# The next tile's score products set singly between value products, instead of in a block

## The reference

```python
def _L0_xattn_ref(q, k, v, Wq, bq, Wk, bk, Wv, bv):   # q: 256x512, k = v = context: 25088x512
    qp = einsum('bsd,ed->bse', q, Wq) + bq            # 256 x 128
    kp = einsum('bsd,ed->bse', k, Wk) + bk            # 25088 x 128
    vp = einsum('bsd,ed->bse', v, Wv) + bv
    z = sigmoid(einsum('bqe,bke->bqk', qp, kp) / sqrt(128))
    return einsum('bqk,bkd->bqd', z, vp)

x = x + _L0_xattn_ref(_layernorm(x), ctx_1024, ctx_1024, ...)
x = x + _L0_attn_ref(_layernorm(x), ...)
x = x + _L0_ffn_ref(_layernorm(x), ...)
```

## Time and profile before

| | us |
|---|---|
| median of 3 runs | 576.66 (576.39 to 577.11) |
| the profiled execution | 576.42 |
| its span, first to last instruction | 574.6 |
| PE busy | 569.0 (99%) |
| PEld busy | 477.3 (83%) |
| DVE busy | 456.3 (79%) |
| ACT busy | 402.2 (70%) |
| granted TensorE clock | 1.000 |

### The profile page before, as it was taken

How to read it: one execution, slowest core, us unless ns; L and a number is a source line. 1 busy time by engine, 2 the same in 40 slices (tenths; PEclk the granted TensorE clock), 3 DMA queues, 4 the chain that set the end, 5 groups by cost and what they waited for, 6 DMA issues and landing times.

```text
span 574.6 us, 8074 instructions
## 1 busy us (share of the span) xinstructions
PE 569.0 (99%) x3010; PEld 477.3 (83%) x3010; DVE 456.3 (79%) x494; ACT 402.2 (70%) x542; POOL 1.7 (0%) x7
## 2 busy tenths in 40 slices
PE   8999999999999999999999999999999999999998
PEld 5888888888888888888888888888888887877887
DVE  6987878787878797879788988787878798887742
ACT  6776767676767787778777787776777784697321
POOL 1000000000000000000000000000000000000000
PEclk9999999999999999999999999999999999999999
DMA  9667787767677877787678777677687742100201
GB/s 329 224 198 244 236 248 228 230 216 244 211 233 243 265 244 229 248 270 243 222 254 254 249 230 256 219 222 223 216 277 236 221 147 110 38 1 2 75 0 38
DMA packets 33239, 115.90 MB, mean 202 GB/s; under 512 B 4080, under 2 KB 4784, under 8 KB 32944
## 3 DMA queue, kind: packets, MB, share of 16 engines
q1 hardware_dynamic: 32768, 115.05, 63.2%
q10 hardware_dynamic: 432, 0.33, 0.2%
HBM read 114.84 MB, written 0.52 MB: 201 GB/s over the span
## 4 chain that ended last, share of the span: by engine, by line
PE 96%; ACT 2%; DVE 1%; issue 0%; POOL 0%; POOLq 0%
PE ps L959 95%; ACT w L548 1%; PE ps L1042 0%; PE ps L1208 0%; PE ps L1295 0%; DVE zl L652 0%; ACT zh L384 0%; PE ps L1167 0%; DVE aTs L847 0%; DVE st L737 0%; DVE sm_s L824 0%; DVE x_s L735 0%; PE ps L1177 0%; ACT zf L415 0%; ACT qk L384 0%
## 5 line engine op out<-in xcount | busy, mean ns | idle before, releaser
L959 PE MATMUL ps<-nh,zh 128*128 128x512 f32 x388 | 142.7, 390 | 0.0
L959 PE MATMUL ps<-nh,zl 128*128 128x512 f32 x388 | 142.6, 389 | 0.1
L959 PE MATMUL ps<-nl,zh 128*128 128x512 f32 x388 | 142.5, 389 | 0.0
L652 DVE TENSOR_TENSOR zl<-zf,zh 128x1024 fp32r<-128x1024 f32 x49 | 60.1, 1226 | 80.5 <-ACT zh L384 80.5
L642 DVE TENSOR_TENSOR nl<-rawn,nh 128x1024 fp32r<-128x1024 f32 x96 | 114.2, 1220 | 0.9 <-issue 0.5
L631 DVE TENSOR_TENSOR tl<-rawt,th 128x1024 fp32r<-128x1024 f32 x96 | 113.0, 1217 | 0.8 <-ACT th L384 0.7
L384 ACT ACTIVATE nh<-rawn 128x1024 fp32r<-128x1024 f32 x96 | 100.4, 1057 | 13.2 <-DMA rawn<-in_ctxn 12.6
L384 ACT ACTIVATE th<-rawt 128x1024 fp32r<-128x1024 f32 x96 | 96.2, 1053 | 1.0 <-DMA rawt<-in_ctxt 1.0
L415 ACT ACTIVATE zf<-ps 128x512 f32<-128x512 f32 x98 | 58.4, 598 | 54.5 <-PE ps L959 48.7
L959 PEld LDWEIGHTS ps<-nh,zl 128*128 128x128 f32 x388 | 72.8, 188 | 15.6 <-DVE zl L652 0.5
L959 PEld LDWEIGHTS ps<-nh,zh 128*128 128x128 f32 x388 | 72.6, 188 | 15.4 <-ACT zh L384 0.4
(11 more groups left out here) (176 smaller groups left out, 613.8 us busy)
## 6 DMA issues: line engine op xcount, KB each, us to landing
rawn<-in_ctxn SPq DMA_DIRECT2D x97, 512.0 KB, 6.6
rawt<-in_ctxt SPq DMA_DIRECT2D x96, 512.0 KB, 5.0
h_s<-in_wg SPq DMA_DIRECT2D x4, 512.0 KB, 6.8
h_s<-in_wu SPq DMA_DIRECT2D x4, 512.0 KB, 7.3
wds<-in_wd SPq DMA_DIRECT2D x4, 512.0 KB, 4.0
raw<-in_ctxt SPq DMA_DIRECT2D x2, 512.0 KB, 8.7
h_s<-in_wvt SPq DMA_DIRECT2D x2, 512.0 KB, 7.3
wq_s<-in_wq SPq DMA_DIRECT2D x1, 1024.0 KB, 10.6
```

The source lines that it names most:

```text
L652: e.tensor_tensor(zl[b % 2][:], zf[:], zh[b % 2][:], ALU.subtract).then_inc(*s.zl.mark(b))
L959: return e.matmul(o, w, x, start=start, stop=stop)
```

## The change

The block `scores(b)` goes out of the loop. Instead `values(b)` issues the score products of tile b + 1 singly: one after each of its last twelve value products, in the same order as before (quarter h, then i). The semaphore waits go with them (`score_waits`), and so do the marks of s. The mark av now comes with the last value product, one score product before the end of the pairs. The last tile's scores keep their block. No product, load, transfer or buffer is added or taken away.

```diff
+            def score_waits(b, i, j):
+                if (i, j) == (0, 0):
+                    e.wait_ge(*s.kph.of(b))
+                    e.wait_ge(*s.zf.of((b - 1, 1)))
+                if (i, j) == (2, 0):
+                    e.wait_ge(*s.kpl.of(b))
+
             def scores(b):
-                e.wait_ge(*s.kph.of(b))
-                e.wait_ge(*s.zf.of((b - 1, 1)))
                 for j in range(4):
                     for i in range(3):
-                        if (i, j) == (2, 0):
-                            e.wait_ge(*s.kpl.of(b))
+                        score_waits(b, i, j)
                         m = score(b, i, j)
                     if j % 2:
                         m.then_inc(*s.s.mark((b, j // 2)))
@@ in values(b), in the loop over j = 2, 3, r = 0, 1, i = 0, 1, 2
                             m = value(b, j, r, i)
-                m.then_inc(*s.av.mark(b))
+                            if (j, r, i) == (3, 1, 2):
+                                m.then_inc(*s.av.mark(b))
+                            if b < NB - 2:
+                                k, h = i, 2 * (j - 2) + r
+                                score_waits(b + 1, k, h)
+                                m = score(b + 1, k, h)
+                                if (k, h % 2) == (2, 1):
+                                    m.then_inc(*s.s.mark((b + 1, h // 2)))
@@ the loop over the tiles
             for b in range(1, NB - 1):
-                scores(b)
                 keys(b + 1)
                 if b < NB - 2:
                     values(b)
```

## The result

The changed kernel takes 580.34 us (579.97 to 580.49), before 576.66: the ratio is 1.006, 95% interval 1.0048 to 1.0071. It is 3.7 us slower. The profiled execution has a span of 578.5 us where before had 574.6. It lies inside the stated range, but not in the case that I held likeliest; it is the rival "the wide products never recover their rhythm", for which the text had worked out 580.7.

A forecast was written before the change was run, and what follows sets the result against it. The tensor engine's own rhythm, 9.62 us a tile, was taken as the bound. Profiled 576.42 us + 0 for the pairs + 0.5 for the start stall = 576.9, or 577.2 against the median; stated 577.1, range 573.0 to 581.2.

The forecast's parts named there:

- the case that I held likeliest: Whole kernel: pairs cost what the blocks did, only the start stall adds; 575.9 to 577.4 us, chance 0.47 including case 3.
- the wide products never recover their rhythm: Mixed half: single scores keep values at 233.3 ns, pair 353.3, +3.8 us, 580.7 with the stall; slower, chance 0.31.
- What bounds the kernel: Whole stream: only the tensor engine's own rhythm counts, 9.62 us a tile; any added stall shows in full.
- Part 1, the pair: Mixed halves of 47 tiles, 564 value-score pairs: each costs 346.7 ns as before, so 0 us.
- the short distance is 113 and the value behind it takes 233: Step pricing one pair from rows at block ends: 346.7 ns, exactly the 226.7 + 120.0 of before.
- The bounds, 340.0 and 355.0: Limits in ns for one pair in the mixed half: -3.8 to +4.7 us over 564 pairs.
- The forecast's own sign: Mixed half: the forecast is wrong if the pair differs from 346.7 ns by more than 2 ns.
- Faster, the loads are hidden: Mixed half: score 113.3 and value 226.7, pair 340.0 ns, -3.8 us, 573.2 with the stall; chance 0.20.
- Case 3: Wide products behind each score block: the 0.03 us tail vanishes too, -0.9 us, 576.0 with the stall; inside the forecast's 0.47.
- The estimate from figures: Pair by the skill page's formulas: load 106.7 ns, products 109 and 216, pair 325 ns in either order, change worth 0.
- Part 2, the waits: Scores' waits moved 2.7 us earlier: slack from tile 2 on; in tile 0 a wait on DVE's low keys, 0.53 us once.
- Part 3, the marks: Moved marks: end-of-values about 1.3 us later at no cost; first sigmoid sooner, worth nothing as rounding awaits the second mark.

The follow-up runs named there:

- first: Changed kernel, except that tile 1's scores stay a block behind tile 0's values (no start stall): 579.2 us, ratio 1.0041.
- third: Changed kernel with tile 1's scores as a block and the three products of each value sum in another order: 579.4 us, ratio 1.0043.
- eleventh: Changed kernel with tile 1's scores as a block; mixed half has its first two scores together, then single ones, a value last: 581.31 us, ratio 1.0076.
- twelfth: Changed kernel with tile 1's scores as a block; one score behind every second value from the eighth, last three scores at the end: 580.07 us, ratio 1.0053.
- seventh: Kernel before with 32 unused bytes per partition ahead of all tiles of the stream, moving its operands together: 576.75 us, ratio 0.9999.
- eighth: Kernel before with 32 unused bytes ahead of zh and zl alone, shifting the value products' weights against their streams: 583.88 us, ratio 1.0122.
- sixth: Changed kernel with tile 1's scores as a block; mixed half in groups of six values, then six scores: 577.49 us, ratio 1.0015.
- second: Changed kernel with tile 1's scores as a block; mixed half in groups of two values, then two scores: 576.74 us, ratio 0.9996.
- fifth: Changed kernel with tile 1's scores as a block; mixed half in groups of three values, then three scores: 577.4 us, ratio 1.0015.

## Why the prediction was right or wrong

**What bounds the kernel: right.** The stream is PE's own rhythm and nothing else; a change of 6.7 ns in the distance of two products shows in full in the kernel's time, and so does a stall of half a microsecond.

**Part 1, the pair: wrong by 6.7 ns, and with it the point forecast.** The step that failed is "the short distance is 113 and the value behind it takes 233". I took the row for the first score of a block and the row for the first wide product behind a block, and set them side by side as if each pair began from the settled state in which those rows stand. The first pair does: 113 and 232. The two behind it, of the same sizes, come to 118 and 241, 120 and 236, before the row starts again; that they begin from what the pair before left is my reading of it. Pairs in a row are a state of their own, 353.3 ns on the mean, that no row of before shows. The forecast's own sign, a pair within 2 ns of 346.7, says that it was wrong. The bounds, 340.0 and 355.0, held the pair; that the range held the time is owed to the rival that was kept in it, not to the forecast. Why the row has three places no run shows. The rival had the size, 353.3, but its parts were off: 233.3 and 120.0 there, 236.3 and 117.0 on the mean here. Its period of 9.70 was 0.02 too high, because the keys behind the last pair recover with one dear product (236) and not with five: they gave 19 ns back.

**The rivals.** "Faster, the loads are hidden" is out: a score did cost 113 to 120, so up to seven nanoseconds were won there, and 5 to 14 were lost at the value behind. The loss stands where the text said against this rival that it would, at the value whose load has only the score's time. Case 3, the tail of 0.03 us vanishes, happened (2.75 to 2.73) and is no more than a quarter of the loss in the half before it. The chances were too much on the forecast: 0.31 on what came.

**The estimate from figures.** By the figures of the Trainium skill, page "TensorE: Matmul & The Clock Gate", sections "LDWEIGHTS (loading the stationary operand)" and "Back-to-back issue gap" (whose N/2.4 + 2.5 it gives for an isolated product), the estimate was 0 for the change as well, a pair of 325 ns in either order. The runs show that the missing part is not a constant: 226.7, 233 and 241 ns for the same instruction. Of loads two ahead, which would have favoured the faster rival, the runs show nothing: in all of them a load starts with the product before its own.

**Part 2, the waits: right.** 0.56 us in tile 0 against 0.53, at the place and by the releaser named; no wait for keys in any later tile.

**Part 3, the marks: right, but for what it didn't ask.** The first sigmoid of a tile starts sooner, the second where it did. The timeline of ACT in the kernel after (a tile without extra work), against the earlier trace rows:

```profile
314.93 0.60 ACT L415 ACTIVATE zf<-ps 128x512 f32<-128x512 f32 x1 [0.79 <-PE ps L959]
317.05 0.60 ACT L415 ACTIVATE zf<-ps 128x512 f32<-128x512 f32 x1 [1.52 <-PE ps L959]
317.68 1.06 ACT L384 ACTIVATE zh<-zf 128x1024 fp32r<-128x1024 f32 x1
```

The two sigmoids, back to back before, now stand 2.1 us apart, and the rounding waits for the second, so nothing is won. The stall of 0.44 us at 309 us came by another way, through the scalar engine's queue. The chain of waits of the kernel after, in order of time:

```profile
296.93 8.31 DMA rawn<-in_ctxn
...
305.26 0.05 ACT nh L384
305.31 0.92 issue
306.23 1.05 ACT wuh L384
307.28 0.98 ACT zf L415 x2
308.25 0.02 issue
308.28 1.07 ACT zh L384
```

A context transfer took 8.31 us where the two before it took 6.6 and 6.9; the tile also has an up-projection's copy (wuh) in ACT's queue ahead of the sigmoids, so zh and zl came late. Four kernels with the same or a longer period (first, third, eleventh, twelfth) have no such stall, and the seventh, with the order of before, has one of 0.18 us at 307.6. The eighth, also with the order of before, has one of 0.34 us, and its chain of waits has the same links, a late context transfer and an expert's copy ahead of the sigmoids:

```profile
259.91 8.48 DMA rawn<-in_ctxn
...
269.38 1.04 ACT wgh L385
270.43 0.98 ACT zf L416 x2
...
273.81 1.20 PE ps L960 x4
```

So such a stall needs no change of the order. I hold this one for a late transfer and not for an effect of the change; that is argued, since no run moved the transfers. Whether the timed runs of the changed kernel contain it can't be read from them; 2.76 + 0.56 = 3.3 us of the 3.7 are explained without it.

**What stays open.** The eighth run shows that the offset between the weights and the stream sets the distance; that load and stream meet in memory is argued. The kernel after shows by itself that one order at one set of addresses has two rhythms (347 in tile 0, 353.3 in all others). That offset and rhythm are one mechanism is argued, not shown: no run changed the offset under the mixed order. Nor did any run put a tile of the steady stream into the 346.7 rhythm; two entries were tried, and only the stall within the mixed half of tile 0 led there. A stall among the values ahead of the mixed half, in the tile at 309.46, did not.

## What to carry to other kernels

Where the tensor engine has no idle time, a product's price is the distance of starts in the very sequence in which it will stand; the price of an alternation can't be put together from the ends of two blocks, and the bounds must stay as wide as those ends. Narrow products between wide ones are not free cover for weight loads: singly they cost 7 to 11 ns each over a tile here (up to 14 where the row is settled), in twos no more in all than the block. When an engine has slack on the mean, look at the first tile: a wait moved forward was free in 46 tiles and cost 0.56 us in one. And compare the offsets of weights and stream within 64 bytes before any reordering; 32 bytes cost this kernel 1.2%, twice the change studied.

## What the runs showed of the hardware

- In an unbroken stream of value products of 512 fp32r columns, each with a weight load beside the one before, the distance settles at 226.7 ns at the full granted clock if weights and stream start at the same offset within 64 bytes or 4 bytes apart; at 230 to 233.9 ns at the eight other offsets tried (8 to 60 bytes). Moving all operands of the stream by 32 bytes together changed nothing in it. The wide products of the late layers took 229 ns at a like offset and 233.3 at 32 bytes apart.
- A single narrow product (256 columns) between wide ones can settle in more than one rhythm with the same instructions: 347 or 353.3 ns a pair. After a block of six or twelve scores the wide products took 5 of their kind (233, 236, 229, 232, 231) to come back to 226.7; behind the pairs of the kernel after it was one (236), behind those of the eleventh run eight of the first nine. After the wait at the first value of tile 0 it differed between kernels: none in the kernel after and the sixth, four in the kernel before (236, 228, 232, 231), nine in the second and fifth.
